# Second attention's first step: who issues its moves, and in what order

## The chip, the cores and the metric

The kernel runs on one core of a Trainium2 chip. The metric is the device time of one execution in microseconds (us), as the median of three runs. One further execution was taken with the hardware profiler; every row below comes from it, with times in us from the start of its span.

## The reference, cut to what matters

A residual stream x of 4096 tokens by 256 features passes four layers, each with a layer norm ahead of it:

```python
x = x + L0_xattn(layernorm(x), ctx)   # 16 heads of 16, 77 keys per batch, mask, biases
x = x + L0_ffn(layernorm(x))          # 6 experts, top 2 of a router, gelu
x = x + L1_xattn(layernorm(x), ctx)   # 16 query heads, one shared key and value head
x = x + L1_ffn(layernorm(x))          # 256 -> 1024 -> 256, fixed point, piecewise linear gelu
```

The change concerns the beginning of the third of them:

```python
c = concat([mem, kv], axis=1)                 # both are ctx here
qh = (q @ w_q) split into 16 heads
attn_prob = softmax(qh @ k.T / 4)
out = (attn_prob @ v) joined @ w_concat
```

and one weight of the fourth: `h = x @ w1 + b1`, where the kernel works with the rows of w1 less its first row, and the first row of w1 (`mlp_w1_0`) is subtracted from the others on the chip.

## The kernel before, in words

The tokens are worked in blocks of 512 (N), 8 blocks to a layer (BLOCKS). The attention steps are numbered through: G = 0 to 7 are the first attention, G = 8 to 15 the second. Features lie in two halves of 128 partitions (c = 0, 1). Each float32 product is made of leading and remaining parts: `qh` and `ql` are the two parts of the queries, made from a PSUM bank by ScalarE (`leading`, line 305) and VectorE (`rest`, line 332).

A score matmul (`score`, line 413) contracts over a stack of rows, `qst`, that holds qh twice (partitions 0 to 31 and 32 to 63), ql (64 to 95) and, in the second attention, the negated maxima `mt` (96 and 97). The stack has two slots, used in turn. It is filled by DMA within the on-chip memory, with one semaphore for each half c (`stacked[c]`) and one for the maxima (`mt_stacked`):

- `stack_queries(eng, G, c)`: two moves qst<-qh (line 254) and one qst<-ql (line 257), 256 KB each.
- `stack_maxima(eng, G)`: one move qst<-mt (line 262), 32 KB, after ScalarE has copied the turned maxima (`maxima`, line 310).

In each step G TensorE computes the scores of G and, between them, the queries of block G + 1 (line 141) and 16 score matmuls for its maxima (`max_unit`, line 388), which VectorE reduces (line 342). Unit u uses half c = (u % 4) // 2, so units 2 and 3 are the first to need the second half of qh. `leading` of block G + 1 overwrites qh, and so it waits until `stacked[c]` of block G has landed. The first score of a step waits for `mt_stacked` and `stacked[0]`; score 8 waits for `stacked[1]`.

The order of work is written out by hand for each engine. Nearly all DMAs are issued by SyncE (SP) from its own queue; ScalarE (ACT) issues a few at the very beginning. Between the experts (second layer) and step 8 there is a border, where the queries and maxima of block 8 are made without a step around them. There SP issues, in this order: the queries' first half, the maxima, the queries' second half, then it waits until the experts have added all their outputs (`ex.added`), and issues the load of the first weight row, broadcast to 128 partitions (`ff.row0`, 512 KB, line 963) and of the last bias (`ff.rows`, 1 KB, line 964). Then the steps' moves follow, for each step both halves of the queries of block G + 1 and then its maxima.

GpSimd (POOL) waits for `ff.row0` in step 8, subtracts it from both parts of the weight (line 1075, twice, with a small memset between), and only then goes on to what stands behind in its queue: the layer norm's power for step 9 (line 103), the remaining parts of the outputs (line 284). ScalarE scales the shifted weight in step 9 (line 1242).

Of the kernel before, what the change touches and what calls it, by code (L numbers as in the profile page):

```python
# [16 lines left out]
P = 128  # L17
N = 512
NT = N // P
BLOCKS = B * S // N  # L20
C = D // P
# [3 lines left out]
F = 1024  # L25
# [815 lines left out]
def build(nc, d, out):  # L841
    m, at0, at1 = memory_map()
    place = Places(nc)
    with ExitStack() as stack:
# [10 lines left out]
        att = Attention(nc, sem, place, norm, ps, m)  # L855
        l0, l1 = Layer(place, "l0_", True, at0), Layer(place, "l1_", False, at1)
        ex = Experts(nc, sem, place, norm, ps, m)
        ff = FeedForward(nc, sem, place, norm, ps, m)
# [8 lines left out]
        def rows_of(w):  # L867
            return w.rearrange("(c p) n -> p c n", p=P)
# [25 lines left out]
        with nc.Block() as block:  # L894
            @block.sync
            def _(sp):
                sp.dma_start(x[:, 0:NT, :], d["x"][:, 0:NT, :]).then_inc(x0_in, 16)
                sp.dma_start(ident[:], d["ident"]).then_inc(q_in, 16)
                sp.dma_start(wq0, rows_of(d["wq0"])).then_inc(q_in, 16)
                sp.dma_start(klowf[96:P, :, :], d["low"]).then_inc(c_in, 16)  # L900
                sp.dma_start(id5f[:], d["ident5"]).then_inc(c_in, 16)
                att.load_mask(sp, 0, d["mask"])
                sp.dma_start(x[:, NT:2 * NT, :], d["x"][:, NT:2 * NT, :]).then_inc(x1_in, 16)
                sp.dma_start(x[:, 2 * NT:4 * NT, :], d["x"][:, 2 * NT:4 * NT, :]).then_inc(x2_in, 16)

                att.stack_low(sp, 0)
                sp.wait_ge(kst_clear, 1)
                sp.wait_ge(kt_ready, 1)
                for c in range(C):
                    for par in range(2):  # L910
                        for k, part in enumerate((l0.kh, l0.kl, l0.kh)):
                            sp.dma_start(l0.kst[32 * k + 16 * par:32 * k + 16 * par + 16, c * HC + par:(c + 1) * HC:2, :].bitcast(F32),
                                         part[64 * par:64 * par + 64, c, :].bitcast(F32)).then_inc(kst_in[c], 16)
                    if c == 0:
                        att.stack_queries(sp, 0, 0)
                att.stack_maxima(sp, 0)
                att.stack_queries(sp, 0, 1)
                att.load_mask(sp, 1, d["mask"])
                for b in range(2, B):
                    tiles = slice(2 * b * NT, 2 * (b + 1) * NT)  # L920
                    sp.dma_start(x[:, tiles, :], d["x"][:, tiles, :]).then_inc(xr_in, 16)

                for G in range(BLOCKS):
                    n = G + 1
                    if n < BLOCKS:
                        att.stack_low(sp, n)
                        for c in range(C):
                            att.stack_queries(sp, n, c)
                        if n + 1 < BLOCKS:
                            att.load_mask(sp, n + 1, d["mask"])  # L930
                        att.stack_maxima(sp, n)
                    if G == 1:
                        sp.wait_ge(wql_ready, 1)
                        sp.wait_ge(wol_ready, 1)
                        sp.wait_ge(v_done, 2)
                        sp.dma_start(ew1, rows_of(d["moe_w1"])).then_inc(ex.w1_in, 16)
                    if G == 2:
                        sp.wait_ge(v_done, 2)
                        sp.wait_ge(id5_ready, 1)
                        sp.wait_ge(kst_const, 2)  # L940
                        sp.dma_start(ex.projf[:], rows_of(d["proj"])).then_inc(ex.small_in, 16)
                        sp.dma_start(ex.anchors[:], d["anchors"]).then_inc(ex.small_in, 16)
                        sp.dma_start(ex.tempc[:], d["temp"]).then_inc(ex.small_in, 16)
                    if G == 6:
                        sp.dma_start(ex.w2raw[:], d["moe_w2"]).then_inc(ex.w2_in, 16)

                sp.wait_ge(ex.w1_ready, 1)
                for dst, name in ((wk1, "wk1"), (wv1, "wv1"), (wq1, "wq1"), (wo1, "wo1")):
                    sp.dma_start(dst, rows_of(d[name])).then_inc(l1_in, 16)
                sp.wait_ge(l1_clear, 3)  # L950
                sp.wait_ge(kl1_ready, 1)
                for par in range(2):
                    for k, part in enumerate((l1.kh, l1.kl, l1.kh)):
                        sp.dma_start(l1.kst[32 * k + 16 * par:32 * k + 16 * par + 16, par, :].bitcast(F32),
                                     part[64 * par:64 * par + 64:4, 0, :].bitcast(F32)).then_inc(kst1_in, 16)
                sp.wait_ge(wl1_ready, 2)
                sp.wait_ge(k1_done, 1)
                sp.dma_start(fw1, rows_of(d["mlp_w1"])).then_inc(ff.w1_in, 16)
                att.stack_queries(sp, BLOCKS, 0)
                att.stack_maxima(sp, BLOCKS)  # L960
                att.stack_queries(sp, BLOCKS, 1)
                sp.wait_ge(ex.added, ALL_EXP)
                sp.dma_start(ff.row0[:], d["mlp_w1_0"].to_broadcast([P, F])).then_inc(ff.row0_in, 16)
                sp.dma_start(ff.rows[:], d["mlp_b2"]).then_inc(ff.rows_in, 16)

                for G in range(BLOCKS, 2 * BLOCKS):
                    n = G + 1
                    if n < 2 * BLOCKS:
                        for c in range(C):
                            att.stack_queries(sp, n, c)  # L970
                        att.stack_maxima(sp, n)
                    if G == BLOCKS + 3:
                        sp.wait_ge(ff.w1_ready, 4)
                        sp.dma_start(fw2, d["mlp_w2"]).then_inc(ff.w2_in, 16)

                for g in range(BLOCKS):
                    sp.wait_ge(ff.added, 2 * (g + 1))
                    sp.dma_start(out[:, g * NT:(g + 1) * NT, :], x[:, g * NT:(g + 1) * NT, :]).then_inc(ff.stored, 16)
                sp.wait_ge(ff.stored, 16 * BLOCKS)
# [134 lines left out]
            def _(act):  # L1114
# [96 lines left out]
                    att.leading(act, BLOCKS, c)  # L1211
                norm.norm(act, LN_ATT1 + 1)
                att.maxima(act, BLOCKS, FIRST_MAX1[0])
                for c in range(C):
                    norm.lead(act, LN_ATT1 + 1, c, att.W[c], att.xh)

# [38 lines left out]
                for k in range(BLOCKS * FC):  # L1255
                    g, c = divmod(k, FC)
# [530 lines left out]
```

## Time and profile before

| | |
|---|---|
| median of 3 runs | 789.33 us (789.02 to 789.87) |
| the profiled execution | 787.69 us, of which the span 785.5 us |
| TensorE busy | 729.2 us (93% of the span) |
| VectorE busy | 644.6 us (82%) |
| ScalarE busy | 514.0 us (65%) |
| GpSimd busy | 373.0 us (47%) |
| DMA through SP's queue (q1) | 46.54 MB |
| DMA through ACT's queue (q10) | 1.24 MB |

The span runs from the first to the last instruction on the profiled core. A busy share is an average over four layers with different limits, so for a change at one place the wait that ends last at that place is what counts. The chain that ended last names it.

### The profile page before, as it was taken

How to read it: one execution, taken by the hardware profiler on the slowest of the kernel's cores; microseconds unless marked ns; L12 is line 12 of the kernel's file. 1: busy time of each engine (PE TensorE's matmuls, PEld its weight loads, DVE VectorE, ACT ScalarE, POOL GpSimd, SP SyncE). 2: the span in 40 equal slices, each digit the busy share in tenths (PEclk: the TensorE clock that was granted, in tenths of full speed). 3: DMA queues.
4: the chain of work that ended last, by engine and by line, in shares of the span. 5: the costliest groups of instructions: out<-in, count | busy, mean ns of one | idle time of the engine just before them, and what ended most of it. 6: DMA issues, size and time to landing. Idle time of an engine off the chain costs nothing.

```text
span 785.5 us, 13554 instructions
## 1 busy us (share of the span) xinstructions
PE 729.2 (93%) x4372; PEld 549.3 (70%) x4372; DVE 644.6 (82%) x1546; ACT 514.0 (65%) x943; POOL 373.0 (47%) x323
## 2 busy tenths in 40 slices
PE   4799999999999999999997999999989999999995
PEld 3566666766558888888874555555568888888985
DVE  7648778777878878888897888998788999999995
ACT  3446556565654456555436777677778989989885
POOL 6374444334222223232214232232259999999884
PEclk9889999999999999999999999999999999999999
DMA  7975634654210000001029665755200000000001
GB/s 234 134 209 121 139 76 93 119 120 88 68 36 1 1 1 7 1 1 55 1 41 143 89 82 76 131 76 77 30 1 1 2 28 28 28 28 2 28 28 54
DMA packets 25101, 48.64 MB, mean 62 GB/s; under 512 B 3686, under 2 KB 7016, under 8 KB 24520
## 3 DMA queue, kind: packets, MB, share of 16 engines
q1 hardware_dynamic: 23366, 46.54, 30.6%
q10 hardware_dynamic: 1666, 1.24, 0.5%
q8 instruction: 36, 0.59, 0.3%
q14 instruction: 33, 0.27, 0.1%
HBM read 12.12 MB, written 4.19 MB: 21 GB/s over the span
## 4 chain that ended last, share of the span: by engine, by line
PE 54%; DVE 19%; issue 8%; ACT 7%; DMA 7%; POOL 4%; SPq 0%; ACTq 0%; DVEq 0%; POOLq 0%
PE bank L141 15%; PE bank L649 6%; PE bank L436 6%; PE bank L413 6%; DMA qst<-mt 5%; PE bank L424 5%; PE bank L388 5%; DVE mx L342 4%; PE bank L416 3%; DVE fpart L768 3%; PE bank L812 3%; PE bank L391 2%; DVE x L617 2%; DVE fyl L780 2%; DVE ffixed L762 2%
## 5 line engine op out<-in xcount | busy, mean ns | idle before, releaser
L316 ACT ACTIVATE pt<-bank 77x512 f32<-77x512 f32 x256 | 141.1, 589 | 78.2 <-PE bank L416 58.3
L342 DVE TENSOR_REDUCE mx<-bank 128x4 f32<-128x308 f32 x256 | 109.0, 471 | 22.5 <-PE bank L391 12.3
L413 PE MATMUL bank<-qst,l_kst 128*77 128x512 f32 (+1 forms) x256 | 102.8, 417 | 15.8 <-DMA qst<-mt 9.8
L721 POOL TENSOR_TENSOR frise<-fg,fg 128x512 f32<-128x512 f32 x64 | 101.3, 1583 | 6.7 <-ACT fg L739 1.5
L388 PE MATMUL bank<-l_kblk,qh 128*128 128x308 f32 x256 | 81.3, 336 | 10.1 <-DVE mx L342 5.7
L284 POOL TENSOR_TENSOR ol<-ot,oh 128x512 fp32r<-128x512 f32 x32 | 41.4, 1294 | 94.4 <-ACT oh L321 50.2
L617 DVE SCALAR_TENSOR_TENSOR x<-bank,eweight,x 128x256 f32<-128x256 f32 x192 | 79.6, 477 | 4.1 <-PE bank L649 3.8
L413 PEld LDWEIGHTS bank<-qst,l_kst 128*77 128x77 f32 (+1 forms) x256 | 36.5, 146 | 65.1 <-ACT pt L316 24.1
L103 POOL TENSOR_TENSOR rstd<-var,minus_half 128x4 f32<-128x4 f32 x32 | 34.4, 1076 | 100.1 <-DVE var L98 52.2
L114 ACT ACTIVATE xn<-x,shift,rstd 128x256 f32<-128x256 f32 (+1 forms) x128 | 67.2, 594 | 17.1 <-POOL shift L105 17.1
L388 PEld LDWEIGHTS bank<-l_kblk,qh 128*128 128x128 f32 x256 | 48.0, 192 | 42.8 <-issue 33.1
L812 PE MATMUL bank<-fw2h,fyh 128*128 128x256 f32 x256 | 73.4, 287 | 4.8 <-DVE fyl L780 4.6
L728 POOL TENSOR_TENSOR fy<-fpart,fg 128x512 f32<-128x512 f32 x48 | 68.5, 1428 | 9.8 <-DVE fpart L768 6.8
L812 PE MATMUL bank<-fw2l,fyh 128*128 128x256 f32 x256 | 72.0, 281 | 0.0
L812 PE MATMUL bank<-fw2h,fyl 128*128 128x256 f32 x256 | 71.8, 281 | 0.0
L424 PE MATMUL bank<-pt,l_vall 128*32 128x512 f32 x512 | 68.2, 604 | 1.3 <-DVE ut L347 0.9
L768 DVE SCALAR_TENSOR_TENSOR fpart<-ffixed,frise 128x512 f32<-128x512 uint16 x64 | 58.2, 911 | 11.2 <-POOL frise L721 11.2
L518 POOL TENSOR_TENSOR ehl<-eh,ehh 128x512 fp32r<-128x512 f32 x16 | 20.7, 1293 | 80.6 <-ACT ehh L534 80.6
L649 PE MATMUL bank<-ew2h,ehh 128*128 128x256 f32 x192 | 55.8, 291 | 2.9 <-DVE x L617 2.9
L532 ACT ACTIVATE eh<-bank 128x512 f32<-128x512 f32 x48 | 28.7, 598 | 41.5 <-PE bank L141 40.5
L812 PEld LDWEIGHTS bank<-fw2h,fyh 128*128 128x128 f32 x256 | 48.2, 188 | 10.8 <-DVE fyl L780 8.9
L649 PE MATMUL bank<-ew2l,ehh 128*128 128x256 f32 x192 | 54.1, 282 | 0.0
(176 smaller groups left out, 2117.0 us busy)
## 6 DMA issues: line engine op xcount, KB each, us to landing
qst<-qh SPq DMA_DIRECT2D x64, 256.0 KB, 6.5
qst<-ql SPq DMA_DIRECT2D x32, 256.0 KB, 8.8
out<-x SPq DMA_DIRECT2D x8, 512.0 KB, 2.6
qst<-ml SPq DMA_DIRECT2D x8, 480.0 KB
x<-in_x SPq DMA_DIRECT2D x3, 1024.0 KB, 12.4
weights<-in_mlp_w SPq DMA_DIRECT2D x2, 1024.0 KB, 5.0
mraw<-in_mask SPq DMA_DIRECT2D x8, 154.0 KB
x<-in_x SPq DMA_DIRECT2D x2, 512.0 KB, 5.8
```

The source lines that it names most:

```text
L141: last = self.nc.tensor.matmul(out, w, a, start=(first and k == 0), stop=(k == len(ops) - 1))
L316: self.nc.scalar.activation(self.pt[0:T, i // 4 % 2, i % 4, :], self.bank_of(G, i)[0:T, :], ACT.Exp).then_inc(self.probs, 1)
L342: self.nc.vector.reduce_max(out, banks[u % len(banks)][:, 0:4 * T].rearrange("q (p par t) -> q p par t", p=2, par=2), AX.X).then_inc(self. ...
L388: last = self.nc.tensor.matmul(bank, self.qh[:, c, tile], keys, start=True, stop=not layer.masked)
L413: last = self.nc.tensor.matmul(out, layer.kst[rows, layer.stack(c * HC + 2 * k + par), b * T:(b + 1) * T], self.qst[rows, self.slot(G), c ...
L424: last = self.nc.tensor.matmul(self.U[32 * k:32 * k + 32, :], layer.vall[:, self.batch(G), layer.value(c * HC + 2 * k + par), :], self.pt[ ...
L617: last = self.nc.vector.scalar_tensor_tensor(tile, part, self.weight[:, g % 2, 2 * k + t, e:e + 1], tile, ALU.mult, ALU.add)
L649: last = self.nc.tensor.matmul(self.OUT[k][:, t * D:(t + 1) * D], a[:, e % self.R, tile], w[:, e, :], start=(j == 0), stop=(j == 2))
L721: self.nc.gpsimd.tensor_tensor(self.rise[:, k % 2, :], self.g1[:, k % self.R, :], self.g0[:, k % self.R, :], ALU.subtract).then_inc(self.r ...
L728: self.nc.gpsimd.tensor_tensor(self.y[:, k % 2, :], self.part[:, k % 2, :], self.g0[:, k % self.R, :], ALU.add).then_inc(self.y_ready[0], 1)
L768: self.nc.vector.scalar_tensor_tensor(self.part[:, k % 2, :], self.fractions[:, k % self.R, :, 0], 2.0 ** -16, self.rise[:, k % 2, :], ALU ...
L812: last = nc.tensor.matmul(self.OUT[2 * (g % 2) + t // 2][:, t % 2 * D:(t % 2 + 1) * D], a[:, k % self.R, t * P:(t + 1) * P], w[:, c, :], s ...
```

## The change

Three moves in the hand-written order. The second half of the queries of block 8 is issued right behind the first. The maxima of block 8 are issued by ScalarE from its own queue, right behind the copy that makes them and ahead of two copies of the next block's norm (`norm.lead`, line 132). The loads of the first weight row and of the last bias are issued behind the six query moves of block 9 and ahead of its maxima, instead of ahead of all of them. Nothing is added or removed otherwise.

```diff
@@ SyncE
-                att.stack_queries(sp, BLOCKS, 0)
-                att.stack_maxima(sp, BLOCKS)
-                att.stack_queries(sp, BLOCKS, 1)
+                for c in range(C):
+                    att.stack_queries(sp, BLOCKS, c)
                 sp.wait_ge(ex.added, ALL_EXP)
-                sp.dma_start(ff.row0[:], d["mlp_w1_0"].to_broadcast([P, F])).then_inc(ff.row0_in, 16)
-                sp.dma_start(ff.rows[:], d["mlp_b2"]).then_inc(ff.rows_in, 16)
 
                 for G in range(BLOCKS, 2 * BLOCKS):
                     n = G + 1
                     if n < 2 * BLOCKS:
                         for c in range(C):
                             att.stack_queries(sp, n, c)
+                        if G == BLOCKS:
+                            sp.dma_start(ff.row0[:], d["mlp_w1_0"].to_broadcast([P, F])).then_inc(ff.row0_in, 16)
+                            sp.dma_start(ff.rows[:], d["mlp_b2"]).then_inc(ff.rows_in, 16)
                         att.stack_maxima(sp, n)
@@ ScalarE
                 norm.norm(act, LN_ATT1 + 1)
                 att.maxima(act, BLOCKS, FIRST_MAX1[0])
+                att.stack_maxima(act, BLOCKS)
                 for c in range(C):
                     norm.lead(act, LN_ATT1 + 1, c, att.W[c], att.xh)
```

## Rows read from the trace of the kernel before

**Rows 1.** The page: shares of the chain that ended last, by engine.

```profile
PE 54%; DVE 19%; issue 8%; ACT 7%; DMA 7%; POOL 4%; SPq 0%; ACTq 0%; DVEq 0%; POOLq 0%
```

**Rows 2.** The chain from border to step 9: start us, us, what.

```profile
411.59 0.60 ACT mt L310
412.20 0.68 SPq L262
...
414.24 6.85 DMA qst<-ql
...
421.17 0.61 ACT qh L305
...
432.64 2.92 DMA qst<-mt
```

**Rows 3.** Timeline of TensorE: start us, us, operation, count, idle before and its releaser.

```profile
415.60 0.67 PE L413 MATMUL bank<-qst,l_kst 98*77 98x512 f32 x2 [1.67 <-issue]
...
421.82 0.41 PE L388 MATMUL bank<-l_kblk,qh 128*128 128x308 f32 x1 [2.05 <-ACT qh L305]
...
435.60 0.68 PE L413 MATMUL bank<-qst,l_kst 98*77 98x512 f32 x2 [0.92 <-DMA qst<-mt]
```

**Rows 4.** Timeline of ScalarE, border and steps 8 and 9.

```profile
412.08 0.57 ACT L132 ACTIVATE xh<-bank 128x512 fp32r<-128x512 f32 x1
...
421.17 0.60 ACT L305 ACTIVATE qh<-bank 128x512 fp32r<-128x512 f32 x1 [2.40 <-DMA qst<-ql]
...
439.06 0.60 ACT L305 ACTIVATE qh<-bank 128x512 fp32r<-128x512 f32 x1 [0.28 <-PE bank L141]
```

**Rows 5.** Timeline of SyncE's DMA issues, border and steps 8 and 9.

```profile
402.49 1.27 SPq L254 DMA_DIRECT2D qst<-qh  x2
404.00 0.55 SPq L257 DMA_DIRECT2D qst<-ql  x1
...
414.89 0.59 SPq L963 DMA_DIRECT2D frow<-in_mlp_w  x1
...
438.37 1.21 SPq L254 DMA_DIRECT2D qst<-qh  x2
...
441.58 0.61 SPq L257 DMA_DIRECT2D qst<-ql  x1
```

**Rows 6.** Windows: length, busy time of each engine, granted clock, DMA share, GB/s.

```profile
0.00:7.10 7.10, 0.00 (x0) 0.00 (x0) 5.28 (x5) 1.28 (x1) 2.46 (x8) 1.00 0.77 235
...
409.40:413.40 4.00, 2.85 (x23) 2.33 (x22) 3.65 (x10) 1.07 (x2) 0.00 (x0) 1.00 0.00 0
...
420.50:421.75 1.25, 0.00 (x0) 0.00 (x0) 0.00 (x0) 0.58 (x2) 0.00 (x0) 1.00 0.96 356
...
433.85:434.80 0.95, 0.83 (x7) 0.14 (x1) 0.95 (x2) 0.89 (x3) 0.00 (x0) 1.00 0.12 35
...
439.40:451.50 12.10, 11.43 (x72) 6.77 (x71) 10.87 (x24) 9.46 (x19) 3.88 (x3) 1.00 1.01 131
```

**Rows 7.** Moves issued from 440.3 to 442.3: issue to landing.

```profile
DMA to landing us min/median/max: 8.4/9.9/11.1
```

**Rows 8.** DMA issues from ACT's queue at the start: KB each, us to landing.

```profile
ctx<-in_ctx ACTq DMA_DIRECT2D x1, 308.0 KB, 5.2
...
weights<-in_wk ACTq DMA_DIRECT2D x1, 256.0 KB, 4.8
...
hsel<-in_headsel ACTq DMA_DIRECT2D x1, 4.0 KB, 5.4
```

**Rows 9.** Timeline of ScalarE's DMA issues at the start.

```profile
1.73 0.49 ACTq L1117 DMA_DIRECT2D hsel<-in_headsel  x1
```

**Rows 10.** Timeline of GpSimd in steps 8 and 9, and ScalarE's scaling in step 9.

```profile
423.23 2.37 POOL L1075 TENSOR_TENSOR weights<-weights,frow 128x1024 f32<-128x1024 f32 x1 [4.13 <-DMA frow<-in_mlp_w]
425.66 0.94 POOL L1078 MEMSET frow<- 1x1024 f32 x1
...
440.78 1.29 POOL L284 TENSOR_TENSOR ol<-ot,oh 128x512 fp32r<-128x512 f32 x1 [1.81 <-ACT oh L321]
...
446.06 0.62 ACT L1242 ACTIVATE weights<-weights 128x512 f32<-128x512 f32 x1
```

## Prediction

> **What bounds the kernel, and how I read it.** The page comes first: TensorE, busy 93% of the span, carries 54% of the chain that ended last; DMA has 7% of it [rows 1]. A change to the order of three DMAs can only win where that chain passes through them, so the chain is read next, at the border. It goes through the maxima's copy on ScalarE (411.59), SP's issue of their move (412.20), SP's issues of the queries' second half, then 6.85 us of the move qst<-ql up to 421.1, and ScalarE's copy of the next block's qh at 421.17; later through the move of block 9's maxima, 2.92 us from 432.64 [rows 2]. The engines' timelines show the same place: ScalarE idles 2.40 us for that qst<-ql, TensorE 2.05 us for that qh [rows 3, 4]. Steps 9 and on have no such stall: there qh's second half is copied 3.46 us after the step's first score (439.06 less 435.60), in step 8 5.57 us after it (421.17 less 415.60) [rows 3, 4]. So 2.1 us is the most that an earlier second half wins by itself. The last view is the windows, for how full the DMA engines are, because each of the three edits puts a move where another is under way. TensorE has its full clock here (1.00, the 2.4 GHz level) [rows 6], so no part of the answer lies in the clock.
>
> I follow one quantity: the first score of step 9, at 435.60 now [rows 3]. Everything later hangs on it, one for one, as each step starts with the landing of its maxima. Call the first score of step 8 s (415.60 now).
>
> **Edit 1, the second half at once.** SP has issued the first half by 404.55 [rows 5]; the second half follows at about 404.6, so six moves of 256 KB lie back to back, as in step 9. There the first issue is at 438.37, the data flow from 439.4 to about 451.3 at 131 GB/s (12.10 us times 131 GB/s is 1.58 MB, the six moves), and the last lands at 441.58 + 11.1 = 452.7 [rows 5, 6, 7]. That is data until 12.9 us, landing 14.3 us after the first issue. From 402.49 that gives data until 415.4 and landing at 416.8. The copy of qh then has to be no earlier than 416.8, but it also needs s + 3.46, which is later; the stall is gone. The price is that the DMA engines, idle from 409.4 to 413.4 now [rows 6], are full until 415.4.
>
> **Edit 2, the maxima from ScalarE.** The copy still ends at 412.2, so the issue is not earlier. It takes about the 0.68 us that SP's takes [rows 2]. Behind it on ScalarE stand two copies, the first at 412.08 now [rows 4]; it slips to about 412.9, and the second waits for a transpose of TensorE that ends behind that, so this costs nothing. Without that cover it would cost 0.7 us.
> What the move itself takes: alone, in step 9, it needs 2.92 us and a little, with data from 433.85 to 434.80 at a DMA share of 0.12, which is two of 16 engines, and some 0.8 us from the last byte to TensorE's start [rows 2, 3, 6]. At the border now it is 3.4 us (412.20 to 415.60) with the second half's data starting right behind it. After the change its data would start near 413.5, with 1.9 us of the second half's data still to come on the same engines. Lower bound: it isn't held up, s = 412.2 + 3.0 = 415.2. Upper bound: below, in the rival. My value: full engines move 131/16 = 8.2 GB/s each; if the two queues share, the maxima get half, 4.1 GB/s, for 1.9 us, 7.8 of their 16 KB on each engine. The other 8.6 KB, and what the second half still has there (7.8 KB), go at the free rate of 16.4 KB in 0.95 us [rows 6], 0.95 us more: 416.35. To this 0.8 us if the landing is as quick as now, 1.4 us if it is as slow as behind a full queue (451.3 to 452.7): s from 417.2 to 417.8. Since the sharing may be kinder than equal, I take 417.2.
> Do two queues share at all? The row nearest is the start: a 4 KB load issued from ACT's queue at 1.73 had landed 5.4 us later, at about 7.1 [rows 8, 9]. By then 235 GB/s times 7.1 us, 1.67 MB, had moved [rows 6], and only 564 KB of that lay ahead of it on ACT's queue [rows 8]; the other 1.1 MB was SP's. ACT's queue neither waited for SP's nor went past it. So I count on sharing.
> The Trainium skill, in "DMA: Bandwidth & Descriptors", section "Queues, rings and completion order", states that a DMA's semaphore increment lands only after every earlier write from that DMA engine, across its queues. No row here shows it. By that rule even a maxima move that isn't slowed would have to wait for the writes of the second half begun before it, so the case below in which it lands as early as 415.4 would lose chance to the forecast: 789.9 by the rule, 788.1 if it doesn't bind here.
>
> **Edit 3, the weight row behind block 9's queries.** Step 8 with the stall gone, in terms of s: queries of block 9 are issued at s + 2.77 (438.37 less 435.60), qh's copy is at s + 3.46, and the maxima's issue 11.47 us after it (432.64 less 421.17), at s + 14.93 [rows 2, 3, 5]. Landing freely they would start step 9 at s + 17.9. But the queue is not free by then. The six moves' data end at s + 2.77 + 12.9 = s + 15.7. Behind them now stands the weight row: 524 KB at 356 GB/s, 1.5 us [rows 6], to s + 17.2. The maxima, issued at s + 14.93, stand behind it in the same queue: 0.95 us of data, to s + 18.1, and 0.8 to 1.4 us to land: s + 18.9 to s + 19.5. I take s + 19.0, so 1.1 us of the win is given back. Taken away from the front, the row (issued at 414.89 now [rows 5]) frees nothing on the chain: now the queue runs on from 414.4 and is empty just before the maxima of block 9 need it.
> The row's own reader is GpSimd: it would land near 435.2 instead of 423.2, and the shift takes 2.37 + 0.94 + 2.38 us with gaps, to about 441.1. Behind it on GpSimd are the norm's power (read by ScalarE behind that scaling) and ol (440.78), which slips by 1.5 us and is read near 447; ScalarE scales the weight at 446.06 [rows 10]. The scaling has 5 us to spare, the others more than they lose, so nothing; were the cover gone, the step would end later by what the shift is late, up to 12 us.
>
> **The sum.** s + 19.0 = 417.2 + 19.0 = 436.2, against 435.60: 0.6 us later. In the profiled execution's terms, span 785.5 to 786.1 and 787.7 to 788.3; its own time is 1.6 us under the median, so the median goes from 789.33 to 789.9. That is no change that can be measured: 0.2%, 1.6 us, is about what a measurement of this kernel tells from none.
>
> **The rivals.**
> *A, forecast.* Both maxima moves are late: s from 416.8 to 417.8, step 9 at s + 18.7 to s + 19.4, which is 0.1 us earlier to 1.6 us later: 789.2 to 790.9. Chance 0.53.
> *B, only the second is late.* ScalarE's queue lets 32 KB through quickly: s = 415.4, step 9 at 434.4, 1.2 us won: 788.1. For it, only two engines are needed for 1 us; against it, the rate per engine under load is half the free one. 0.17.
> *C, only the first is late.* The weight row slips between the queries' moves, which are held by something other than the engines (131 against 356 GB/s). 417.2 + 17.9 = 435.1, 0.5 us won: 788.8. 0.10.
> *D, neither.* 415.4 + 17.9 = 433.3, the whole stall won: 2.3 us, 787.0. 0.10.
> *E, slower.* The two engines keep the crowded pace to the end of both transfers: 16 KB of maxima and 15.6 KB of queries at 8.2 GB/s is 3.9 us from 413.5, to 417.4, landing at 418.4; step 9 at 437.5, 1.9 us later: 791.2. It decides once s passes 418.2. For it, the saturated windows never show a faster engine; against it, the others are done at 415.4. 0.08. The remaining 0.02 lie beyond, at either side.
>
> **From these, the numbers.** The time is A's, 789.9. A, B and C hold 0.80, from 787.7 to 790.9; with the edges of D and E I give 787.3 to 791.1. Faster by over 0.2% is D and the lucky edge of B: 0.13. Slower is E, the edge of A and part of the rest: 0.10. Same: 0.77.
>
> **What would show it.** Right: no ScalarE idle before qh's second copy in step 8; DMA share near 1 without a gap from 403.5 to past 415; first score of step 8 near 417, with TensorE idle some 3 us before it; the weight row's data right behind the queries' and the maxima's behind that, TensorE idle 2 us or more before step 9. Wrong: a first score before 416, or step 9 starting 18 us after it; or steps 9 to 15, or the last layer, changing their length, which I take as fixed.

## The result: 0.54% slower

The changed kernel takes 793.02 us (median of 12 runs, 790.98 to 798.73), the kernel before 788.77 us (12 runs beside them): ratio 1.0054, 95% interval 1.0038 to 1.0070, or some 4.3 us. The forecast was 789.9, within 787.3 and 791.1, with 0.10 for slower. Run again on another chip, four times, it gave 792.64 against 788.85, ratio 1.0055 (1.0033 to 1.0077). One execution of the run `warm` below was slow, at 1920 us, and stands in no ratio.

The profiled execution has a span of 790.8 us and a time of 793.0. Of its 5.3 us over before, 1.6 us are there when the maxima of block 8 are copied: at 413.17, before at 411.59 [rows 2]. In the repeat they were copied at 412.53, and `row_back` and `row_back_warm` below, alike up to there, copy them at 413.41 and 412.22, so that part moves from run to run. I therefore count from the start of this copy. The timeline of ScalarE in the changed kernel:

```profile
413.17 0.59 ACT L310 ACTIVATE mt<-bank 16x512 fp32r<-16x512 f32 x1 [4.63 <-PE bank L397]
413.78 0.77 ACTq L262 DMA_DIRECT2D qst<-mt  x1
414.60 0.60 ACT L132 ACTIVATE xh<-bank 128x512 fp32r<-128x512 f32 x1 [0.85 <-ACT mt L310]
...
425.43 0.60 ACT L305 ACTIVATE qh<-bank 128x512 fp32r<-128x512 f32 x1 [1.09 <-PE bank L141]
```

The wait for a DMA ahead of qh's second copy is gone (it was 2.40 us [rows 4]). Yet this copy comes 12.26 us after the maxima's, before 9.58. TensorE's timeline says why, against [rows 3]:

```profile
419.56 1.11 PE L413 MATMUL bank<-qst,l_kst 98*77 98x512 f32 x2 [4.05 <-issue]
...
440.39 0.70 PE L413 MATMUL bank<-qst,l_kst 98*77 98x512 f32 x2 [1.39 <-DMA qst<-mt]
```

The first score of step 8 is 6.39 us behind the copy and not 4.01. Two score matmuls then take 1.11 us and not 0.67. The chain of waits shows the twelve matmuls behind them at 4.73 us, where step 9 of the same kernel needs 2.77:

```profile
420.67 4.73 PE bank L141 x12
...
436.97 3.37 DMA qst<-mt
...
441.09 2.77 PE bank L141 x12
```

Windows of the changed kernel (the last three columns: granted clock, DMA share, GB/s), to set beside [rows 6]:

```profile
415.00:416.00 1.00, 0.51 (x5) 0.27 (x3) 1.00 (x4) 0.66 (x2) 0.00 (x0) 1.00 1.04 123
416.50:417.00 0.50, 0.00 (x0) 0.00 (x0) 0.50 (x2) 0.50 (x1) 0.44 (x2) 1.00 0.63 74
417.00:417.50 0.50, 0.00 (x0) 0.00 (x0) 0.50 (x3) 0.44 (x1) 0.37 (x2) 1.00 0.15 16
417.50:418.00 0.50, 0.00 (x0) 0.00 (x0) 0.50 (x3) 0.00 (x0) 0.00 (x0) 0.97 0.13 16
418.00:418.50 0.50, 0.00 (x0) 0.00 (x0) 0.50 (x2) 0.00 (x0) 0.00 (x0) 0.50 0.07 25
...
424.50:425.50 1.00, 1.00 (x6) 0.82 (x5) 0.08 (x1) 0.07 (x1) 0.00 (x0) 0.85 0.35 133
```

The queries' data fill the DMA engines until about 416.8; then two engines (share 0.13 to 0.15 of 16) work until past 418: the maxima, issued at 413.78. The packets by queue say the same. From 413.70 to 416.79 there are packets of SyncE's queue (q1) alone; all 18 of ScalarE's queue (q10) start from 416.79 on, beside the last of q1 (packets, MB, share of 16 engines):

```profile
q1 hardware_dynamic: 205, 0.38, 104.0%
...
q10 hardware_dynamic: 18, 0.03, 12.5%
q1 hardware_dynamic: 19, 0.01, 6.6%
```

TensorE has had nothing to do since 415.5. Near 418 its granted clock goes from 1.00 to 0.50, from 2.4 to 1.2 GHz, and it comes back between 424.5 and 425. Last, GpSimd and VectorE in step 9 of the changed kernel, from both timelines:

```profile
443.00 2.39 POOL L1075 TENSOR_TENSOR weights<-weights,frow 128x1024 f32<-128x1024 f32 x1
445.47 1.01 POOL L103 TENSOR_TENSOR rstd<-var,minus_half 128x4 f32<-128x4 f32 x1
446.56 0.20 POOL L105 TENSOR_TENSOR shift<-minus_mean,rstd 128x4 f32<-128x4 f32 x1
446.83 1.28 POOL L284 TENSOR_TENSOR ol<-ot,oh 128x512 fp32r<-128x512 f32 x1
```

```profile
446.83 0.33 DVE L353 RECIPROCAL rden<-ut 128x32 f32<-128x32 f32 x1
447.20 1.47 DVE L355 TENSOR_TENSOR o<-ut,rden 128x512 f32<-128x512 f32 x1
448.59 0.85 DVE L342 TENSOR_REDUCE mx<-bank 128x4 f32<-128x308 f32 x2
```

VectorE's product at line 355 takes 1.47 us, and the row of before says 0.69:

```profile
442.36 0.69 DVE L355 TENSOR_TENSOR o<-ut,rden 128x512 f32<-128x512 f32 x1
```

It lies beside ol of GpSimd (to 448.11), which before ran from 440.78 to 442.07 [rows 10], ahead of the product. The product ends 0.56 us after ol does, so it hardly advanced while ol ran. The repeat shows it too (1.58 us). The other 15 products of the changed kernel take 0.69 us, and none of them lies beside an ol.

The account, from the copy of block 8's maxima to the issue of block 10's (line 262, at 458.69, 45.52 behind the copy; before 41.57):

| us | changed less before |
|---|---|
| first score of step 8: 6.39 less 4.01 | +2.38 |
| first score to qh's second copy: 5.87 less 5.57 | +0.30 |
| to the issue of block 9's maxima: 11.54 less 11.47 | +0.07 |
| issue to first score of step 9: 3.42 less 2.96 | +0.46 |
| step 9 to the issue of block 10's maxima: 18.30 less 17.56 | +0.74 |
| sum | +3.95 |

The second line hides two amounts. Free of the stall that stretch is 3.46 us (step 9 of before), so the stall's 2.11 us are won, and the 2.41 us from 3.46 to 5.87 are lost. Of these, 0.44 us are the two score matmuls and 1.96 us the twelve behind them, all at the low clock. `warm` below tests that it is the clock.

### The profile page after: what moved, and what is told of

It reads as the page before. It is cut to its first block, busy times and chain, and to the rows that moved or that the text cites. A ratio compares the mean times of both kernels' runs of the same rounds, so it can differ in the third digit from the quotient of the medians.

```text
span 790.8 us, 13554 instructions
## 1 busy us (share of the span) xinstructions
PE 730.2 (92%) x4372; PEld 548.3 (69%) x4372; DVE 646.1 (82%) x1546; ACT 513.2 (65%) x943; POOL 373.3 (47%) x323
## 4 chain that ended last, share of the span: by engine, by line
PE 54%; DVE 19%; issue 9%; ACT 7%; DMA 6%; POOL 4%; ACTq 0%; DVEq 0%; POOLq 0%
PE bank L141 16%; PE bank L649 7%; PE bank L413 6%; PE bank L436 6%; DMA qst<-mt 5%; PE bank L424 5%; PE bank L388 4%; DVE mx L342 4%; PE bank L416 3%; PE bank L812 3%; DVE fpart L768 2%; DVE x L617 2%; PE bank L391 2%; DVE fyl L780 2%; POOL fy L728 2%
```

## The experiments

Each run is read in two ways: its time against the kernel before on the same chip, and the marks of the table below, in us from the copy of block 8's maxima. A time is a median of 4 to 12 executions; the marks are of one profile each, and differ by up to 0.3 us between the changed kernel and its repeat.

| kernel | first score, step 8 | qh's second copy | first score, step 9 | issue of block 10's maxima | ratio to before (95%) |
|---|---|---|---|---|---|
| before | 4.01 | 9.58 | 24.01 | 41.57 | |
| changed | 6.39 | 12.26 | 27.22 | 45.52 | 1.0054 (1.0038 to 1.0070) |
| changed, repeat | 6.11 | 12.37 | 26.91 | 45.27 | 1.0055 (1.0033 to 1.0077) |
| act_idle | 4.25 | 10.20 | 24.64 | 42.21 | 1.0009 (0.9993 to 1.0024) |
| sp_fifo | 7.00 | 13.07 | 27.59 | 45.20 | 1.0030 (1.0018 to 1.0043) |
| row_only | 4.06 | 9.87 | 24.29 | 42.54 | 1.0023 (1.0013 to 1.0034) |
| row_back | 6.18 | 11.11 | 25.64 | 43.25 | 1.0032 (1.0020 to 1.0044) |
| warm | 6.30 | 9.74 | 25.48 | 44.65 | 1.0036 (1.0024 to 1.0049) |
| warm_both | 6.49 | 9.90 | 25.64 | 43.24 | 1.0029 (1.0017 to 1.0040) |
| row_back_warm | 7.06 | 10.50 | 25.06 | 42.68 | 1.0007 (0.9998 to 1.0015) |
| split | 4.60 | 9.64 | 24.17 | 41.78 | 0.9992 (0.9984 to 1.0001) |
| split_warm | 4.96 | 8.43 | 22.92 | 40.53 | 0.9983 (0.9975 to 0.9992) |
| split_one | 4.05 | 7.64 | 22.05 | 39.62 | 0.9968 (0.9956 to 0.9980) |

### Whose queue, or whose data? act_idle and sp_fifo

Theory Q: the maxima were late because the queries' data lay ahead of them on the DMA engines, whichever queue they come from. Theory S: ScalarE's queue is slow to begin. `act_idle` is before with:

```diff
@@ SyncE
                 att.stack_queries(sp, BLOCKS, 0)
-                att.stack_maxima(sp, BLOCKS)
+                sp.wait_ge(norm.xh_ready, C * (LN_ATT1 + 1) + 1)
                 att.stack_queries(sp, BLOCKS, 1)
@@ ScalarE
                 att.maxima(act, BLOCKS, FIRST_MAX1[0])
+                att.stack_maxima(act, BLOCKS)
```

> The maxima of block 8 go from ScalarE's queue as in the change, but onto idle DMA engines: the queries' second half is issued only behind them (about 1 us later than before), and the weight row stands where it stood. Theory Q (the maxima were late because the queries' data filled the DMA engines): data begin about 1.3 us after the issue and the first score comes 3.0 to 3.5 us after the issue, 0.6 us later than before at most; the stall on qh's second copy grows by about 1 us; time 0 to 1.5 us above before. Theory S (ScalarE's queue is slow to begin, whatever the load): first score 5.8 us after the issue as in the changed kernel, step 8 begins over 2 us late, the TensorE clock falls, and the time is 3 us or more above before.

From issue to first score it took 3.63 us (5.78 in the changed kernel, 3.40 before), and the windows show two engines at work between 414.0 and 415.1. A window cut at 414.2 has nothing ahead of it, so the data begin 1.4 us after the issue at 412.79:

```profile
412.80:414.00 1.20, 1.20 (x12) 1.20 (x11) 0.85 (x3) 0.39 (x1) 0.00 (x0) 1.00 0.00 0
414.00:415.10 1.10, 0.51 (x5) 0.28 (x3) 1.10 (x4) 0.76 (x2) 0.00 (x0) 1.00 0.10 30
```

In the changed kernel the same 32 KB began 3.0 us after their issue and took some 1.5 us, not 0.9. Theory S is out. `sp_fifo` is before with SyncE's order changed to both halves, then the maxima:

```diff
-                att.stack_queries(sp, BLOCKS, 0)
-                att.stack_maxima(sp, BLOCKS)
-                att.stack_queries(sp, BLOCKS, 1)
+                for c in range(C):
+                    att.stack_queries(sp, BLOCKS, c)
+                att.stack_maxima(sp, BLOCKS)
```

> The queries' second half at once, the maxima behind it but from SyncE's queue, the weight row where it stood. Theory Q: the maxima's data begin only when the queries' data end, as in the changed kernel; step 8 begins 1.5 to 2.4 us late, the TensorE clock falls to 1.2 GHz for some us, and the time is 2.5 to 3.5 us above before. Theory S: no slow queue, so the first score comes about 3.5 us after the issue, the stall is gone, and the time is 1 to 2 us below before.

First score 7.00, clock fallen (score to qh's second copy 6.07), time 2.4 us above before (1.4 to 3.4): theory Q. It took 6.39 us from issue to score, longer than the 5.78 of the changed kernel. This is no advantage of ScalarE's queue: `row_back_warm` below, with the maxima in that queue, has its first score at 7.06. What these two share is the weight row, issued 2.9 us after the copy, close to the maxima.

### The weight row: row_only and row_back

`row_only` is before with the third edit alone, `row_back` the changed kernel without it.

```diff
@@ row_only, SyncE (row_back takes these lines out of the changed kernel and puts them back ahead of the loop)
                 sp.wait_ge(ex.added, ALL_EXP)
-                sp.dma_start(ff.row0[:], ...)
-                sp.dma_start(ff.rows[:], ...)
...
+                        if G == BLOCKS:
+                            sp.dma_start(ff.row0[:], ...)
+                            sp.dma_start(ff.rows[:], ...)
```

> Only the weight row's place is changed. If the late row costs by itself (GpSimd's shift pushed under VectorE's work of step 9, VectorE's product at line 355 stretched from 0.7 to 1.5 us): 0.7 us above before, with the first score of step 9 unmoved within 0.5 us, and the loss inside step 9. If the row's place is the main cause of the loss: 3 us or more above before. If it costs nothing: within 0.3 us of before.

> The changed kernel with the weight row back in its old place. Theory Q with clock: step 8 begins 2.4 us late, the clock falls, step 9 begins about 2.8 us late, and nothing is lost inside step 9, so 2.8 us above before and about 1.2 us below the changed kernel. If the row's place is the main cause: within 1 us of before or below it.

Alone, the row's place costs 0.28 us up to step 9 and 0.69 us within it, where line 355 is stretched again:

```profile
442.96 1.42 DVE L355 TENSOR_TENSOR o<-ut,rden 128x512 f32<-128x512 f32 x1
```

By time it is 1.8 us (1.0 to 2.7), more than the 0.97 of the one profile; the marks stop at block 10's maxima, and what came behind them was not followed up. `row_back` comes to 43.25, 1.68 us over before and 2.27 under the changed kernel; by time 2.5 us over before (1.6 to 3.5). Its step 9 takes 17.61 us to block 10's maxima, about before's 17.56, and line 355 takes 0.69 us. So the late row is not the main cause, but it is no free edit: about 1 to 2 us of the 4.3.

### The clock: warm, warm_both, row_back_warm

```diff
@@ warm: the changed kernel, TensorE, behind the border's last transposes
+                for k in range(14):
+                    nc.tensor.matmul(ps[7][:, :], l1.wqh[:, 0, 0:P], att.qh[:, k % C, :], start=True, stop=True)
@@ warm_both: also ahead of step 9's first score
+                    if G == BLOCKS + 1:
+                        need(pe, att.probs, att.exp_before(G, 0))
+                        for k in range(8):
+                            nc.tensor.matmul(att.bank_of(G, 0)[:, :], l1.wqh[:, 0, 0:P], att.qh[:, k % C, :], start=True, stop=True)
```

> The changed kernel with 14 filler matmuls (128x512, about 0.23 us each, into a bank that the first score overwrites) on TensorE between the last transpose of the border and the first score; their results are not used. Theory: of the loss, 2.4 us is the TensorE clock, which fell to 1.2 GHz after 4 us without work. Then the clock stays at 2.4 GHz, the first score of step 8 comes as late as before this edit (about 6 us after the maxima's issue), the block of 12 matmuls behind it takes 2.75 us and not 4.7, and the time is about 2 us below the changed kernel. Rival: the matmuls are slow for another reason (a semaphore, the weights' reads) and the time doesn't move by more than 0.5 us.

The maxima are as late as in the changed kernel (6.30), but the twelve matmuls take 2.74 us, qh's second copy is 3.44 us behind the first score, and step 9 begins 1.74 us sooner. Then the gain is lost again, in the chain of waits:

```profile
418.96 2.74 PE bank L141 x12
...
433.28 4.16 DMA qst<-mt
437.48 0.70 PE bank L413 x2
438.18 3.88 PE bank L141 x10
```

(The view ends at 442 us and so shows ten of the last twelve.) With step 8 short, block 9's maxima stand behind the queries and the weight row (4.16 us, alone 2.92), TensorE idles 2.16 us, and over 437.40 to 440.50 its mean granted clock is 0.61. By time `warm` is only 1.4 us under the changed kernel (1.0036 against 1.0054), not the 2 us expected. Hence the second set of fillers.

> As the run with fillers, and 8 more filler matmuls ahead of step 9's first score (into that score's bank; results not used), since with one filler the clock fell there instead, after 2.2 us of idle time. Theory (the clock fall costs 1.5 to 2.4 us wherever TensorE idles over 2 us): the clock stays at 2.4 GHz in steps 8 and 9, step 9 begins as with one filler, the maxima of block 10 are issued 43.8 us after the copy of block 8's maxima and not 44.7 to 45.5, and the time is about 0.9 us below the run with one filler, 1.7 us below the changed kernel, so still 2 us above before: the late maxima, the queue and GpSimd. Rival (no clock effect on the time): same as the changed kernel.

> The changed kernel with the weight row in its old place and the 14 fillers. What is left of the change is the second half at once and the maxima behind it from ScalarE. Theory: maxima 2.2 us late, stall of 2.1 us gone, clock kept: step 9 begins within 0.3 us of before, nothing lost inside step 9, and the time is within 0.5 us of before. Rival: the clock isn't what cost; the time stays 2.5 us above before, as without fillers.

`warm_both` is at 43.24, below the 43.8 expected: the collision at line 355 didn't occur either (0.69 us), so it hangs on how two engines happen to lie. Its first score of step 8 (6.49) follows the fillers without a gap, so there the fillers held it and not the maxima. In time the step from `warm` is small (0.0007, inside both intervals); the marks carry it, not the times. With the clock kept in both steps the change still costs 2.3 us by time (1.3 to 3.2).

`row_back_warm` is the forecast's case with edits 1 and 2 alone and the clock kept: 0.6 us over before (from 0.2 under to 1.2 over), `row_back` without fillers 2.5 us. The marks give 0.57 us of this difference; another 1.2 us lies ahead of the copy in the two profiles, where the kernels are alike, so the times may overstate what the fillers did. Its first score was 7.06, not 6.2, and 1.49 us of idle time was left ahead of it. The weight row's issue lies closer to the maxima there, 2.9 us after the copy against 3.7 in `row_back` (`row_back_warm`, then `row_back`):

```profile
415.13 0.35 SPq L962 DMA_DIRECT2D frow<-in_mlp_w  x1
...
417.12 0.35 SPq L962 DMA_DIRECT2D frow<-in_mlp_w  x1
```

With the row issued 2.9 us after the copy the first score is at 7.00 or 7.06 (`sp_fifo`, `row_back_warm`), with it later or elsewhere at 6.11 to 6.39 (`row_back`, `warm`, the changed kernel and its repeat). That two transfers at once slow the maxima fits this, but no run changed it alone.

### Versions for speed: split, split_warm, split_one

If the maxima wait for what lies ahead of them, only so much of the second half should go ahead as is done by then. `split` issues both qst<-qh moves early, `split_one` only the first:

```diff
@@ split_one: before, SyncE
                 att.stack_queries(sp, BLOCKS, 0)
-                att.stack_maxima(sp, BLOCKS)
-                att.stack_queries(sp, BLOCKS, 1)
+                sp.wait_ge(att.qh_ready, C * BLOCKS + 2)
+                for k in range(2):
+                    if k == 1:                     # split: k == 2, behind the loop
+                        att.stack_maxima(sp, BLOCKS)
+                    sp.dma_start(att.qst[32 * k:32 * k + 32, att.slot(BLOCKS), PAIRS:2 * PAIRS, :].bitcast(F32),
+                                 att.qh[:, 1, :].bitcast(F32)).then_inc(att.stacked[1], 16)
+                sp.wait_ge(att.ql_ready, C * BLOCKS + 2)
+                sp.dma_start(att.qst[64:96, att.slot(BLOCKS), PAIRS:2 * PAIRS, :].bitcast(F32),
+                             att.ql[:, 1, :].bitcast(F32)).then_inc(att.stacked[1], 16)
```

> Before, with only the two qst<-qh moves of the second half issued early; the maxima then qst<-ql follow from SyncE's queue, and the weight row as before. The two early moves' data end near 413.6, when the maxima's data begin. Theory: the first score of step 8 stays within 0.5 us of before, the last ql move lands near 418 and not 421, the stall of 2.1 us on qh's second copy is gone, and the time is 1.5 to 2 us below before. Rival: anything in the queue ahead of the maxima delays them, step 8 begins 1 us or more late, and the time is not below before.

> The split order (two of the second half's three moves ahead of the maxima, all from SyncE's queue) and 9 fillers ahead of step 8's first score. In the split order the first score was 0.6 us late and the clock fell for about 3 us. Theory: with the clock kept, qh's second copy comes 8.1 us after the maxima's copy and not 9.6, step 9 begins 1.5 us earlier than before, and the time is 1.5 us below before, about 787.3. Rival: another wait takes its place, and the time is within 0.7 us of before.

> Before, with only the first of the second half's three moves ahead of the maxima, no fillers. Its data end near 411.6, so the maxima find idle DMA engines: first score 4.0 to 4.2 us after the copy as before, TensorE idle 1.7 us, no fall of the clock. The last move lands near 419.6 and not 421.1, so 1.3 us of the stall of 2.1 us goes. Theory: 1.0 to 1.5 us below before. Rival: the first score slips over 0.5 us or the clock falls, and the time is that of before.

`split`: the first score was 0.6 us late, TensorE idled 2.25 us ahead of it, and the clock fell behind it (mean 0.64 from 416.80 to 421.50, copy 5.04 us behind the score), which ate the stall's gain. My expectation of 1.5 to 2 us was wrong by the same step as the prediction. With nine fillers, `split_warm`, the gain came: 1.3 us (0.6 to 2.0), although the fillers ran up to the first score and held it (4.96, in `split` 4.60). `split_one` needs none. Its chain of waits, with the stall that is left:

```profile
412.09 0.60 ACT mt L310
...
414.03 5.62 DMA qst<-ql
419.73 0.61 ACT qh L305
...
431.19 2.92 DMA qst<-mt
434.14 0.68 PE bank L413 x2
```

TensorE idles 1.72 us ahead of the first score at 416.14 (before 1.67) and keeps its clock; ScalarE waits 0.41 us for the last move and not 2.40. 786.31 us against 788.67, ratio 0.9968, 2.5 us faster (1.6 to 3.5); the marks give 1.95.

The repeat of the changed kernel went with the first of these:

> The changed kernel once more, on the chip of these runs, to stand beside them: 3.5 to 4.5 us above before. In the profile already shown, 1.6 us of 5.3 us had come in the first 90 us, where nothing was changed; expected here: that part differs between runs and is not of the change, while the step from the border to step 10 again loses 3.7 to 4.2 us.

Both came: some 4.3 us by time, and 3.70 us by the marks.

## Why the prediction was wrong

The forecast had step 9 begin 0.6 us later and nothing after it; by the marks it began 3.21 us later, and 0.74 us more were lost inside it. Term by term:

**The stall.** Right: 2.1 us sat there, and ScalarE's wait for the DMA is gone. In `warm`, with the clock kept, the copy is 3.44 us behind the first score, as forecast (3.46).

**The maxima behind the queries' data.** That they would be late was right, the way of it was not, and the size was 0.8 us short. I had s = 417.2 with two queues sharing the engines. Counted from before's copy (1.58 us earlier) it was 417.98. The packets show no sharing with the queries: the maxima's data begin when the queries' end. Sharing or not, the two engines have the same bytes to move; what was too small is the time for them and for the landing. The maxima's data took some 1.5 us, with the two engines at 16 GB/s up to 418.0, half of their free pace (35 GB/s [rows 6]). And from the last data to the first score it was 1.2 us; I had taken 0.8 us from step 9, while step 8 of `act_idle` shows 1.3 us on idle engines.

Two limits of this evidence. In each run with the maxima in ScalarE's queue behind the queries, the last of the six moves was already under way when the maxima's data could have begun. In the changed kernel that is 1.4 us after the issue (as in `act_idle`), at 415.2, and the last move, which takes 2 us at 131 GB/s and ended near 417, began at 415.0. Whether the maxima would pass a move that has not begun, no run shows. And the rule on completion order that the prediction cites from the Trainium skill ("DMA: Bandwidth & Descriptors", section "Queues, rings and completion order") is not tested: the maxima's data were late themselves, and that alone accounts for the landing. Moves issued 0.7 and 1.3 us behind the maxima (`split_one`) left them alone; one with its data under way ahead of them, in either queue, held them back.

**The step that failed: "TensorE has its full clock here, so no part of the answer lies in the clock."** I read the clock of before, where TensorE idles 1.67 us ahead of step 8, and then forecast an idle time of over 3 us there without asking what the clock would do in it. The idle time was 4.05 us, the clock fell to 1.2 GHz, and it cost 2.41 us, which `warm` gives back in step 8 (5.87 to 3.44). This is the largest of the missing terms. Taken off on paper, the marks come to +1.5 us, 790.9 on my median of 789.33, in the range. No run shows that case: in `warm` the queue then took part of it back, and `warm_both`, with the clock kept in both steps, is 2.3 us over before, about 791.6, just over the range. So the clock is the main miss, but not the only one.

**The queue behind the weight row.** The forecast was 1.1 us, the changed kernel shows 0.46. That is not kinder queueing: step 8 was stretched by the slow clock, and the queue had time. In `warm`, with step 8 short, the first score of step 9 comes 4.20 us after the issue, 1.24 us more than before. The term was right under its own assumption.

**GpSimd, "so nothing".** Wrong. I priced the shift's lateness by who waits for its results, and no such wait shows. What cost was the company: the late shift pushed ol beside VectorE's product, which then took twice as long (1.47 us, not 0.69). This product lies on the chain that ended last, and step 9 grew by 0.74 us in the changed kernel and by 0.69 us in `row_only`. In `row_back` and `warm_both`, where the product took 0.69 us, step 9 grew by less than 0.1 us.

**The rivals.** None had the clock, and the measured time lies beyond all of them. E came nearest, with a first score near 418 and two engines that keep the crowded pace, and both were seen. But its loss of 1.9 us was to be all transfer, and the clock's 2.41 us came on top. Of the forecast's own signs of being wrong one came: step 9 changed its length. And one sign of being right did not: TensorE idled 1.39 us ahead of step 9, not 2 us or more.

## What to carry to other kernels

Before a short move is put behind long ones that would be in flight anyway, ask when it must land: in these runs another issuing queue didn't take it past them. When a forecast lengthens an engine's idle time, price the time after it too, by a row in which the clock was low. And a transfer can be too late without anybody waiting for it, if it pushes GpSimd's work beside VectorE's.

## What the hardware showed that I had not expected

The idle time ahead of a matmul did not say by itself whether the granted clock would fall. Idle times of 1.67 to 1.90 us ahead of step 8 left it at 2.4 GHz. Idle times of 2.97 to 4.66 us each brought a stretch at 1.2 GHz, and so did 2.16 us (`warm`, step 9) and 2.25 us (`split`, step 8). But before, `row_only` and `act_idle` idle again in step 8, ahead of the first matmul that needs qh's second half, for 2.05, 2.32 and 2.45 us, and stay at 2.4 GHz. The longest of them, with the window behind it (granted clock 1.00):

```profile
423.02 0.41 PE L388 MATMUL bank<-l_kblk,qh 128*128 128x308 f32 x1 [2.45 <-ACT qh L305]
...
423.00:430.00 7.00, 6.02 (x27) 2.94 (x28) 5.50 (x13) 4.95 (x10) 5.68 (x3) 1.00 1.08 136
```

The other way round, `row_back`, `warm_both` and `split_warm` were granted 0.50 over 412.60 to 413.00, in the border, where TensorE had had no hole of over 1 us since 395. What decides between these cases the runs here don't show. So the expectation of `warm_both` that the clock falls wherever TensorE idles over 2 us does not hold.

VectorE's 128x512 product on on-chip operands took 0.69 us alone and 1.42 to 1.58 us beside GpSimd's 1.28 us subtraction; it took 0.69 us beside GpSimd's 128x4 operations. The 4.05 us hole in the changed kernel, 2.38 us longer than before's, cost as much again behind it: 2.41 us at the low clock.
